# Full fp32 products of a two-layer transformer kernel issued in four column tiles of 32

## The reference

```python
xn = _layernorm(x)
x = x + attention_a(xn) + block_b(xn)     # layer 0: causal attention, 16 heads of 8; block_b is a causal
                                          # attention with norms, then 8 experts 128 -> 512 -> 128, top 2 by gate
xn = _layernorm(x)
x = x + attention_c(xn) + moe_d(xn)       # layer 1: attention without a mask; 8 experts 128 -> 128 -> 128, top 2
```

## Time and profile before

| | |
|---|---|
| median of three runs | 742.12 us |
| profiled execution | 742.59 us |
| its span, first to last instruction | 740.0 us |
| TensorE matmul busy | 711.5 us (96%), 6222 matmuls |
| TensorE weight load busy | 387.6 us (52%), 6222 loads |
| VectorE, ScalarE, GpSimd busy | 569.5, 509.3, 185.2 us |
| mean granted TensorE clock | 0.987 |

### The profile page before, as it was taken

One profiled execution on the slowest core, in us unless ns is written; L12 is line 12 of the kernel. 1 busy time (PEld: TensorE's weight loads), 2 busy tenths in 40 slices (PEclk: granted clock), 3 DMA queues, 4 the chain that ended last, 5 costly groups with the idle time before them and its releaser, 6 DMA issues.

```text
span 740.0 us, 15886 instructions
## 1 busy us (share of the span) xinstructions
PE 711.5 (96%) x6222; PEld 387.6 (52%) x6222; DVE 569.5 (77%) x1127; ACT 509.3 (69%) x632; POOL 185.2 (25%) x425
## 2 busy tenths in 40 slices
PE   5689999999999999999999999999999999999997
PEld 2333345667645665564544456567654666533345
DVE  5989998545788868688999967658778476788966
ACT  7266777366686567667789866764787748588882
POOL 5165546011343012103533200021372110010000
PEclk9699999999999999999999999999999999999999
DMA  6243523000132000004232200031031000030101
GB/s 155 53 140 129 164 93 110 11 19 1 34 96 79 3 25 17 19 5 111 64 88 69 62 3 19 4 99 31 5 93 54 9 11 17 3 94 13 28 25 39
DMA packets 42009, 38.75 MB, mean 52 GB/s; under 512 B 14312, under 2 KB 37232, under 8 KB 41712
## 3 DMA queue, kind: packets, MB, share of 16 engines
q1 hardware_dynamic: 40592, 36.17, 17.5%
q10 hardware_dynamic: 1152, 1.05, 0.6%
q0 software_dynamic: 192, 0.52, 0.3%
HBM read 10.47 MB, written 1.44 MB: 16 GB/s over the span
## 4 chain that ended last, share of the span: by engine, by line
PE 79%; DVE 9%; ACT 4%; DMA 4%; issue 2%; POOL 1%; SPq 1%; ACTq 1%; POOLq 0%; DVEq 0%
PE psum L986 19%; PE psum L973 18%; PE psum L925 15%; PE psum L904 8%; PE psum L877 8%; DVE neg_max L535 6%; PE psum L854 2%; PE psum L935 1%; PE psum L882 1%; DMA inverses<-heads_den 1%; PE psum L857 1%; PE psum L945 1%; PE psum L960 1%; ACT k_stack L716 1%; DVE acc L690 1%
## 5 line engine op out<-in xcount | busy, mean ns | idle before, releaser
L535 DVE TENSOR_REDUCE neg_max<-psum 128x2 f32<-128x1024 f32 (+2 forms) x320 | 344.9, 1113 | 82.2 <-PE psum L877 40.2
L778 ACT ACTIVATE probs<-psum 128x1024 f32<-128x1024 f32 (+1 forms) x320 | 287.1, 938 | 122.4 <-PE psum L904 120.7
L802 ACT ACTIVATE probs<-psum,col 128x512 f32<-128x512 f32 x160 | 100.5, 684 | 78.9 <-PE psum L973 78.3
L925 PE MATMUL psum<-probs,v_ones 128*32 128x512 f32 (+3 forms) x1536 | 152.8, 496 | 0.1
L986 PEld LDWEIGHTS psum<-ew,probs 128*128 128x128 f32 x1024 | 120.1, 192 | 17.6 <-issue 14.2
L986 PE MATMUL psum<-ew,probs 128*128 128x128 f32 x1024 | 129.1, 280 | 0.0
L877 PE MATMUL psum<-k_stack,q_stack 64*128 64x512 bf16 (+3 forms) x768 | 113.7, 333 | 13.6 <-DMA q_stack<-part 8.2
L1071 POOL TENSOR_SCALAR_AFFINE_SELECT probs<-probs 128x512 f32<-128x512 f32 x128 | 82.0, 646 | 176.7 <-ACT probs L778 176.6
L973 PE MATMUL psum<-normed_T_a,ew 128*128 128x512 f32 x256 | 118.0, 599 | 0.0
L904 PE MATMUL psum<-q_stack,k_stack 64*128 64x512 bf16 (+3 forms) x768 | 109.2, 330 | 3.9 <-DVE neg_max L535 1.2
L690 DVE SCALAR_TENSOR_TENSOR acc<-psum,gate,acc 128x128 f32<-128x128 f32 x256 | 71.9, 344 | 23.5 <-PE psum L986 21.7
(11 more groups left out here) (124 smaller groups left out, 494.2 us busy)
## 6 DMA issues: line engine op xcount, KB each, us to landing
q_stack<-part SPq DMA_DIRECT2D x66, 128.0 KB, 2.4
k_stack<-part SPq DMA_DIRECT2D x66, 128.0 KB, 2.4
heads_raw<-head_sums SPq DMA_DIRECT2D x24, 128.0 KB
heads_inv<-inverses SPq DMA_DIRECT2D x12, 256.0 KB, 3.3
ew<-w_expert_in SPq DMA_DIRECT2D x4, 512.0 KB, 4.9
ew<-w_expert_out SPq DMA_DIRECT2D x4, 512.0 KB, 6.7
q_stack<-k_stack SPq DMA_DIRECT2D x14, 128.0 KB, 2.3
q_stack<-maxT SPq DMA_DIRECT2D x48, 32.0 KB, 1.8
```

The source lines that it names most:

```text
L535: eng.tensor_reduce(neg_max[:, q % 2, :, xs[0]:xs[-1] + 1, i], src, AX_X, ALU.max, negate=True).then_inc(vector_done.sem, 1)
L778: eng.activation(dst, src, ACT.Exp, scale=SCALE).then_inc(probs_ready.sem, 1)
L802: ins = eng.activation(probs[:, order.slot[step[:-1]], 2 * k + f, :], two_banks(step)[:, f, :], ACT.Gelu_apprx_tanh if layer else ACT.Gelu ...
L925: ins = eng.matmul(sum_bank[32 * c:32 * c + V_COLS, q0:TILES * P], v_ones[u][:, j, g // 2 * QH + c, col0:col0 + V_COLS], probs[:, order.sl ...
```

## The change

A helper, `columns`, issues a product as four matmuls, one for each group of 32 kept columns. All four read the same moving operand, and each writes its own 32 partitions of the result. Every full fp32 product goes through it, and so does the turn of the maxima, which becomes a plain product of the bf16 parts with the bf16 identity. Its result is therefore fp32 in PSUM (128 x 128 fp32 and no longer bf16), and VectorE's copy converts it to bf16. The other turns (lines 841 and 953), `route_bias`, the scores and the values stay as they are. So do the order, the banks and the semaphores: the last of the four matmuls of the last product signals the step.

```diff
+COLUMN = 32
+COLUMN_TILES = P // COLUMN
...
-                    src = bank(step)[:, 0:P // 2].bitcast(BF16)
+                    src = bank(step)[:, 0:P]
...
+            def columns(dst, kept, moving, start=True, stop=True):
+
+                for c in range(COLUMN_TILES):
+                    some = slice(COLUMN * c, COLUMN * c + COLUMN)
+                    ins = eng.matmul(dst[some, :], kept[:, some], moving, start=start, stop=stop)
+                return ins
...
-                        ins = eng.matmul(dst, proj_qk[:, u, k, :], src[:, :], start=True, stop=True)
+                        ins = columns(dst, proj_qk[:, u, k, :], src[:, :])
...
-                            ins = eng.matmul(dst[:, t * P:(t + 1) * P], src[:, t * P:(t + 1) * P],
-                                             projs[:, u, 0, :], start=True, stop=True)
+                            ins = columns(dst[:, t * P:(t + 1) * P], src[:, t * P:(t + 1) * P], projs[:, u, 0, :])
...
-                    dst = bank(step)[:, 0:P // 2].bitcast(BF16)
+                    dst = bank(step)[:, 0:P]
...
-                    eng.transpose(dst, max_part[:, q % 2].rearrange("p a n c -> p (a n c)"),
-                                  ident16[:, :]).then_inc(work_full.sem, 1)
+                    ins = columns(dst, max_part[:, q % 2].rearrange("p a n c -> p (a n c)"), ident16[:, :])
+                    ins.then_inc(work_full.sem, 1)
...
-                        ins = eng.matmul(dst[:, t * EXPERTS:(t + 1) * EXPERTS], src[:, t * P:(t + 1) * P],
-                                         router[:, layer, :], start=True, stop=True)
+                        ins = columns(dst[:, t * EXPERTS:(t + 1) * EXPERTS], src[:, t * P:(t + 1) * P], router[:, layer, :])
...
-                        ins = eng.matmul(dst[:, f, :], w, normed_T["y" if layer else "a"][:, :], start=True, stop=True)
+                        ins = columns(dst[:, f, :], w, normed_T["y" if layer else "a"][:, :])
...
-                            ins = eng.matmul(dst[:, t * P:(t + 1) * P], middle[:, f, t * P:(t + 1) * P], w,
-                                             start=f == chunks[0], stop=f == chunks[-1])
+                            ins = columns(dst[:, t * P:(t + 1) * P], middle[:, f, t * P:(t + 1) * P], w,
+                                          start=f == chunks[0], stop=f == chunks[-1])
```

More of the change, by code:

```diff
@@ L934, in _ @@
                     for t in range(TILES):
-                        ins = eng.matmul(dst[:, t * P:(t + 1) * P], headsT[:, t * P:(t + 1) * P],
-                                         projs[:, step[2], 1, :], start=True, stop=True)
+                        ins = columns(dst[:, t * P:(t + 1) * P], headsT[:, t * P:(t + 1) * P], projs[:, step[2], 1, :])
                     ins.then_inc(work_full.sem, 1)
```

## The result

The changed kernel takes 733.27 us in the median of four runs (732.85 to 735.84), beside 742.46 us (741.61 to 743.08) for the kernel before in the same session. The ratio is 0.9883 with a 95% interval of 0.9866 to 0.9900: 9.2 us are saved (8.7 us by the ratio). The forecast was 13.1 us saved. The profiled execution took 733.63 us, 731.7 of them the span, 8.3 us shorter than the span before.

What follows compares the result with a forecast made beforehand. TensorE was taken to bound the kernel from 120 us on. Its terms, 9.3 - 2.5 + 4.0 + 5.0 - 0.2 = 15.6 us, with 13.1 us arriving, gave 729 us; own range 725 to 732, with rivals 724 to 740.

Steps and rivals of the forecast that it cites:

- First loads: TensorE runs beginning after another form expose 27 ns of load instead of 107; with smaller items 9.3 us saved.
- ends: On TensorE, 123 more runs end with the last tile's 20 ns delay: 2.5 us lost.
- pitch: 1472 instructions with 128 moving columns (lines 986, 935, 857) at 109 and not 111.7 ns: 4.0 us saved.
- routers: 64 router instructions with 8 moving columns at 33 ns instead of 111: 5.0 us saved, ends 0 and 5.4.
- borders of form: Changes between full and tiled products on TensorE, about 94 ns each: 24 vanish, 26 arise, 0.2 us lost.
- VectorE's copy: Copy of the turned maxima reads fp32, about 284 ns against 218: 3.2 us more on VectorE, 0.5 us of it showing.
- What reaches the end: Of TensorE's 15.6 us, 0.6 arrives from the first 120 us and 13.0 from later; less 0.5, 13.1 us saved.
- the rival of the waits: Half the gain after 120 us goes into waits at lines 877 and 904 for VectorE and ScalarE: 735 us, chance 0.16.
- The floor of short tiles: A router's four short tiles run one after another, costing about 111 ns; the 5.0 us vanish: 734 us, chance 0.11.
- Too few instructions: TensorE cannot be fed every 13.6 ns in line 986 steps; at 16 ns 28 us more, 757 us, chance 0.10.
- Tiles in series: Four tiles with the same moving operand run one after another: 956 us more, about 1685 us, chance 0.03.
- S: Follow-up theory: the gain that did not arrive waits for ScalarE's exponentials, which free the banks of the scores; 5 us.

Runs made afterwards that it cites:

- the pair with both neighbours cut: VectorE's maxima over half the keys and nearly all ScalarE exponentials at half width: 730.07 us on the kernel before, 718.42 us on the changed kernel.
- The two runs of one part alone that lose: Kernel before with only the turn of the maxima in column tiles: 748.68 us; with only the second expert products (line 986) in column tiles: 744.17 us.

## Why the prediction was right and where it was not

- *First loads, ends, pitch, routers, borders of form.* Right. The sum was 15.6 us less of TensorE's time; the changed steps give 14.2 with their own waits in them, 3.7 of it at the routers, where 5.0 were taken (4.6 in the pair with both neighbours cut, from the same comparison). The step of line 986 took 1.88 us (1.89), a single expert-in step between row tiles 1.86 (1.86), a router wave 34 ns (33), the first load 24 ns (27). The two runs of one part alone that lose, +5.9 and +1.4 us, lie beside +6.3 and +1.4 by the same prices. One slip has no weight: the sum takes 111.7 ns for the old pitch and the reading above it 111.5, a difference of 0.3 us.
- *VectorE's copy.* Right in duration (282 ns, 284) and in what shows (0.7 us, 0.5).
- *What reaches the end.* This is the term that was mis-sized. I let 0.6 of the first 1.2 us and a tenth of the following 14.4 be lost, 2.0 in all, and the copy's 0.5. The `max` and `scores` steps took 6.1 back, 3.6 more than these 2.5, and the changed steps gave 1.4 less than their sum. So the forecast of 13.1 became 8.1 by the steps, 8.3 between the profiled spans and 9.2 between the medians. The range held the result, but the time lies nearer to the rival of the waits (735) than to the forecast (729). The mechanism of that step, "meets VectorE's maxima and ScalarE's exponentials sooner: their results free the PSUM banks", is a part of it only: 1.9 us behind the exponentials and, on balance, nothing behind the maxima. The larger part stood in no term: 2.9 us at three waits for transfers and 0.8 at one for GpSimd's split. The size was taken from the chain's 21% outside TensorE, which says how much of the path lies elsewhere now and not how close behind the others are. The trace before had 80.3 us of load waits in 143 pieces for the two results; whether a size could have been read from them was not tried.
- *Where it is lost.* All along the span, but not evenly: by stretch the `max` and `scores` steps give back 1.6 us in the first 120, 2.7 up to 560 and 1.8 behind. The largest single losses are 1.2 us at 113 us, 0.9 at 557, 0.8 at 45 and 0.7 at 343. The rest is small losses and small gains that leave 2.4. The chain of the first, after the change, from 101 us on (start us, us, what):

```profile
101.83 2.58 DMA heads_raw<-head_sums
...
105.09 4.02 DMA inverses<-heads_den
...
109.13 3.64 DMA heads_inv<-inverses
...
112.79 0.76 DVE headsT L559
...
113.59 1.12 PE psum L834 x32
```

and before it, in the kernel before:

```profile
103.59 2.66 DMA heads_raw<-head_sums
...
106.92 3.32 DMA inverses<-heads_den
...
110.25 3.08 DMA heads_inv<-inverses
...
113.35 0.89 DVE headsT L557
...
114.28 1.17 PE psum L935 x8
```

  The chain starts 1.76 us earlier, but its three transfers take 10.24 us and took 9.06, so that 0.69 us arrive at the output projection. The 1.2 us more that they take are no more than the spread of such transfers between traces (above), so it is open whether the change made them longer.
- *The rivals.* The floor of short tiles fell (34 ns). Too few instructions fell: 13.2 ns an instruction for 1.68 us on end, where 15 was the point of decision and 14.5 the densest known. Tiles in series fell. The gain that turns into waits (7 us, 735) came nearest: behind 120 us 4.5 us went into waits, about two thirds of the size that I gave it. But it named VectorE and ScalarE releasing the banks, and less than half of the loss is put to them. Against it stood that the gain falls in expert steps; that did not protect it, since what these steps leave earlier is paid at a later step.
- The clock stood at 1.00 behind 120 us, as forecast.

The Trainium skill, "TensorEngine Tiling (Array Packing)", section PSUM Bottleneck, says that tiling speeds up TensorE but not the emptying of PSUM, which may then become the limit, and advises to use both ScalarE and VectorE for it. The first half agrees with this case in a small part: of the 14.2 us that TensorE's steps gave, 1.9 are given back behind ScalarE's exponentials. The second does not pay here by itself: the copy given to ScalarE cost 5.9 us.

**What stays open.** With both neighbours at half their main work, `max` and `scores` still give back 2.85 us behind 60 us, 1.7 of it at waits for transfers. No run took the transfers out of the path or traced one kernel several times, so how much of the 2.9 us at these places is the change's and how much the single execution's is not known. And S rests on one pair in which the maxima were halved as well.

## What to carry to other kernels

Price a change of form by counting borders in the order as it will stand, not per part: the same edit was worth about -3.5 us among tiled neighbours (-4.2 by the ratios) and +5.9 among full ones. When the bounding engine gets faster by some per cent, list what it waits for beside the engines next to it, transfers and small helpers too: here over a third of what it gained did not reach the end. And before a pair of runs is read for a mechanism, compare the granted clock of their stretches.

## What the hardware showed beside that

- TensorE was fed an instruction every 13.2 ns for 1.68 us, and the instruction transfers grew from 49 packets of 0.80 MB to 95 of 1.56 MB (the first row is before, the second after) with no wait for them in the traces:

```profile
q8 instruction: 49, 0.80, 0.5%
```
```profile
q8 instruction: 95, 1.56, 0.9%
```

- A full fp32 product costs nothing more as four column tiles in this kernel, even with 128 kept columns and one moving operand for all four (1.88 us for the step of 16, against 1.98); with 8 moving columns it costs a third (34 against 111 ns a wave), and its first load exposes a quarter (24 against 102 ns).
- A gap of TensorE can cost more than its length. In the kernel with both neighbours cut and the change, 1.55 us of work in 4 us were followed by a stretch at 0.58 of the clock, and a step of values took 1.93 in place of 1.06 us. The Trainium skill, "TensorE: Matmul & The Clock Gate", Part 1, tells that the lower rate is the default and that activity lifts it; the rows agree, with 1.00 again from 48 us on, behind 4.00 of 4 us busy.
